# Moving DVE's two memory products ahead of the four masked score blocks in every attention tile

## Chip, cores and metric

One NeuronCore of one Trainium2 chip runs the whole kernel. The metric is the device time of one execution in microseconds (us). The engines are named as in the profile: PE (TensorE, matrix products), DVE (VectorE), ACT (ScalarE), POOL (GpSimd) and SP (SyncE, which issues DMAs).

## What is computed

The input is x, 4 batches of 1024 tokens by 256 features. After a layer norm the output is x + attention(xn) + ffn(xn). The feed-forward part is a mixture of 8 experts with two chosen for each token, plus a shared one. The attention has 16 heads of width 16 and mixes two things: causal linear attention inside the sequence, and four "fine" memories with learned norms.

```python
sq = elu1(q); M = fine_memories.sum(0); z = fine_memory_norms.sum(0)
out_coarse = (sq @ M) / clip(sq @ z, EPS)
a_f = einsum('bhsd,mhde->mbhse', sq, fine_memories)
n_f = einsum('bhsd,mhd->mbhs', sq, fine_memory_norms)
w = softmax(n_f.mean(-1), axis=0)
out_fine = (a_f / clip(n_f, EPS) * w).sum(0)
exp_prob = sigmoid(relu(coarse_repr @ eg_w1.T + eg_b1) @ eg_w2.T + eg_b2)
memory_output = exp_prob * out_fine + (1 - exp_prob) * out_coarse
# local_output, in chunks of 128 tokens, with carried S and z:
scores = einsum('bhid,bhjd->bhij', qc, kc) * mask
num = scores @ vc + qc @ S;  den = scores.sum(-1) + qc @ z;  out = num / clip(den, EPS)
output = gate * memory_output + (1 - gate) * local_output;  y = output @ w_o.T
```

## The kernel before

The kernel runs three phases one after the other. A tokens phase does the layer norm, the shared feed-forward part and the routing. An experts phase runs the chosen experts. The attention phase, from about 415 us to the end, works through 32 tiles of 128 tokens: 8 tiles t = 0 to 7 in each of 4 batches b = 1 to 4. A tile is written (b,t) below.

The order of the work in the attention phase is written out by hand in `attention_order()`, as one list of steps (name, b, t, j). Each engine walks the same list and does only its own share of each step. The engines meet through semaphores. `since(engine, semaphore, count)` is a wait, and `then_inc` is a signal at the end of an instruction.

The steps of a tile, in the order of the list, with the lines that do them:

- `scores` 0 to 3: PE multiplies keys and queries of four heads for each block (L1385, issued two blocks at a time). DVE multiplies each block with the causal mask into `probs` (L1632). The block's PSUM bank is free when DVE has read it.
- `fine` 0 and 1, for tile t-1: DVE multiplies half of the memory outputs `with_mem` with their coefficients `coef` into `prod`, which the profile calls `mem_rows` (L1670). POOL then adds the four memories and `rest` up into `att` (L1721 to L1725). PE has no part in it.
- `coarseT`: PE transposes the coarse output (L1402), ACT copies it (L1511).
- `keys`: PE transposes the keys (L1376), ACT copies them (L1496).
- `hidden`: PE (L1407), then ACT (L1515). `oproj` of tile t-2: PE multiplies with w_o (L1397), DVE adds it to `total` (L1678).
- `norms` 0 to 2, for tile t+1: PE multiplies the queries with the memories (L1370, three banks). ACT copies each bank into `with_mem` (L1490), where it waits until DVE's `fine` of tile t-1 has read the same buffer. DVE makes `rn` (L1620, L1622) and `coarse` (L1625) from it.
- `values`: PE multiplies all four blocks of `probs` with the values (L1416), ACT copies the result to `valT` (L1518).
- `gate` (L1433, ACT L1522), `state` (L1438), `local` (L1423, L1428): PE. DVE then makes `den` (L1638, L1640), the local output (L1641), `coef` and `rest` (L1646 to L1658), and folds the state (L1662).
- `outT` of tile t-1: PE transposes `att` (L1393), ACT copies it (L1499) and scales the rows that POOL gathered for the experts (L1506).

"Fill" steps lie between these: the projections q, k and v and the input transposes `xT` of later tiles and of the next batch (PE L88 to L90 and L1345, ACT L1476 to L1485, DVE L1557 to L1580). Which fill stands where depends on t. In tiles t = 0, 4, 5, 6 and 7 of the first three batches (t = 0 in all four) one stands ahead of `hidden`. For t = 2 `v` fills stand ahead of and behind `values`, for t = 1 and 3 one stands behind it; t = 7 also has an `xT` fill ahead of `values`. The tiles t = 4 to 7 of the last batch have no fills.

PE's results go to seven PSUM banks that are used in turn, the ring `a_ring` (`NR = 7`). Every step that writes a bank takes the next one. `use_bank` makes PE wait until the reader of the use seven before has finished. The steps `fine`, `rest`, `fold`, `state`, `split`, `mexp` and `weights` take no ring bank. SP issues the DMAs that lay queries and keys out in `q_st` and `k_st`. These wait for the scores that still read the old content.

Of the kernel before, what the change touches and what calls it, by code (L numbers as in the profile page):

```python
# [1073 lines left out]
def attention_order():  # L1074
    order = [("xT", 1, 1, 0), ("xT", 1, 1, 1)] + [("norms", 1, 0, j) for j in range(NB3)]
    order += [("q", 1, 1, 0), ("q", 1, 1, 1)]
    tiles = [(b, t) for b in range(1, B + 1) for t in range(NT)]
    for i, (b, t) in enumerate(tiles):
        fill = {0: [("k", b, 1, 0), ("split", b, 1, 0), None, ("k", b, 1, 1), ("split", b, 1, 1)],
                1: [None, None, ("v", b, 4, 0)],  # L1080
                2: [None, ("v", b, 5, 0), ("v", b, 6, 0)],
                3: [None, None, ("v", b, 7, 0)]}.get(t, [])
        if b < B:
            a = b + 1
            fill = {3: [None, None, ("v", b, 7, 0), ("xT", a, 0, 0), ("xT", a, 0, 1)],
                    4: [("q", a, 0, 0), ("q", a, 0, 1), ("split", a, 0, 0), ("k", a, 0, 0), None],
                    5: [("k", a, 0, 1), ("split", a, 0, 1), ("v", a, 0, 0)],
                    6: [("v", a, 1, 0), ("v", a, 2, 0), ("v", a, 3, 0)],
                    7: [("xT", a, 1, 0), ("xT", a, 1, 1), None, ("q", a, 1, 0), ("q", a, 1, 1)]}.get(t, fill)
        more = fill + [None] * 5  # L1090
        order += [("scores", b, t, 0), ("scores", b, t, 1)]
        if i:
            order.append(("fine", *tiles[i - 1], 0))
        order += [("coarseT", b, t, 0), ("scores", b, t, 2), ("scores", b, t, 3)]
        if i:
            order.append(("fine", *tiles[i - 1], 1))
        if t == 0:
            order.append(("mean", b, 0, 0))
        order += [("keys", b, t, 0), more[0], ("hidden", b, t, 0)]
        if i > 1:  # L1100
            order.append(("oproj", *tiles[i - 2], 0))
        if i + 1 < len(tiles):
            order += [("norms", *tiles[i + 1], j) for j in range(NB3)]
        if t == 0:
            order.append(("mexp", b, 0, 0))
        order += [more[1], ("values", b, t, 0), more[2], ("gate", b, t, 0)]
        if t < NT - 1:
            order.append(("state", b, t, 0))
        if t == 0:
            order.append(("weights", b, 0, 0))  # L1110
        order += [("local", b, t, 0), ("rest", b, t, 0)]
        if t < NT - 1:
            order.append(("fold", b, t, 0))
        order += more[3:5]
        if i:
            order.append(("outT", *tiles[i - 1], 0))
    order += [("fine", B, NT - 1, 0), ("fine", B, NT - 1, 1), ("oproj", B, NT - 2, 0), ("outT", B, NT - 1, 0),
              ("oproj", B, NT - 1, 0)]
    return [x for x in order if x]


ATT_ORDER = attention_order()

NR = 7
# [714 lines left out]
```

How the kernel before makes its waits and increments, by code:

```python
    def link(ins):  # L98
        links[0] += 1
        ins.then_inc(done, 1)
        eng.wait_ge(done, before + links[0])
# [140 lines left out]
        @block.sync  # L242
# [1 line left out]
            def tokens(u, index):  # L244
                sp.dma_start(x_in[u][:, :, :], x_tok[bass.ds(index, 1), :, :, :]
                             .rearrange("b p t c -> p (b t) c")).then_inc(s_x[u], 16)
            def tails():
                sp.wait_ge(s_tail, 1)
                for e in range(E):
                    at = sp.value_load(tail_i[0:1, e:e + 1], min_val=0, max_val=E * REGION - P)
                    sp.dma_start(d["rows"][bass.ds(at, P), :], filler).then_inc(s_tailed, 16)
            sp.wait_ge(s_x[0], 16)
            tokens(0, 0)
            sp.dma_start(st_g, d["sg_t"].rearrange("(k p) n -> p k n", p=P)).then_inc(s_sw, 16)
            sp.dma_start(st_u, d["su_t"].rearrange("(k p) n -> p k n", p=P)).then_inc(s_sw, 16)
            sp.dma_start(st_d[:, 0:2, :], d["sd_t"][0:2 * P, :].rearrange("(f p) n -> p f n", p=P)
                         ).then_inc(s_sw, 16)
            sp.dma_start(st_d[0:SF[2], 2, :], d["sd_t"][2 * P:FS, :]).then_inc(s_sw, 16)
            for it in range(B // 2):
                for u in range(2):
                    b = it * 2 + (2 + u)
                    sp.wait_ge(s_base, b * 2 * NS)
                    if b == B + 1:
                        sp.wait_ge(s_xst[0], 32)
                        for k in range(KC):
```

## Time and profile before

| | us |
|---|---|
| median of 3 runs | 847.85 |
| lowest and highest run | 846.88, 850.22 |
| the profiled execution | 844.33 |
| its span | 842.4 |
| its granted PE clock, mean | 0.924 |

The span runs from the first to the last instruction of the profiled execution. The granted clock is 1.0 at 2.4 GHz and 0.5 at 1.2 GHz. Busy time of PE is that of pipelined matrix products whose ends are modelled, so it isn't peak use. An idle time in a row is that of the engine just before the instruction, with the operation that ended it. "PEld" rows are PE's weight loads, which run beside its products.

### The profile page before, as it was taken

How to read it: one execution, taken by the hardware profiler on the slowest of the kernel's cores; microseconds unless marked ns; L12 is line 12 of the kernel's file. 1: busy time of each engine (PE TensorE's matmuls, PEld its weight loads, DVE VectorE, ACT ScalarE, POOL GpSimd, SP SyncE). 2: the span in 40 equal slices, each digit the busy share in tenths (PEclk: the TensorE clock that was granted, in tenths of full speed). 3: DMA queues.
4: the chain of work that ended last, by engine and by line, in shares of the span. 5: the costliest groups of instructions: out<-in, count | busy, mean ns of one | idle time of the engine just before them, and what ended most of it. 6: DMA issues, size and time to landing. Idle time of an engine off the chain costs nothing.

```text
span 842.4 us, 17283 instructions
## 1 busy us (share of the span) xinstructions
PE 672.4 (80%) x5154; PEld 566.1 (67%) x5155; DVE 561.4 (67%) x1353; ACT 356.4 (42%) x841; POOL 354.3 (42%) x438
## 2 busy tenths in 40 slices
PE   0689887980696999999678898878988888979884
PEld 0567766770685888888656776767866777757762
DVE  1475574674553555565467788878887788786883
ACT  0654453432332334333433464444644445454441
POOL 1043535355397400000233565355553655435663
PEclk9999999995798999999867999989999899989996
DMA  8107173442484333333325436374473634627210
GB/s 241 50 32 256 68 231 127 159 147 98 138 195 123 94 106 106 100 105 103 97 88 91 111 72 145 106 145 95 80 152 95 144 90 85 154 47 147 73 51 26
DMA packets 79723, 96.27 MB, mean 114 GB/s; under 512 B 15852, under 2 KB 63180, under 8 KB 79660
## 3 DMA queue, kind: packets, MB, share of 16 engines
q1 hardware_dynamic: 69132, 74.93, 34.7%
q0 software_dynamic: 7680, 19.93, 8.3%
q10 hardware_dynamic: 2848, 0.61, 0.4%
q8 instruction: 34, 0.56, 0.3%
q14 instruction: 29, 0.24, 0.1%
HBM read 38.68 MB, written 31.59 MB: 83 GB/s over the span
## 4 chain that ended last, share of the span: by engine, by line
DVE 20%; PE 18%; issue 7%; ACT 4%; POOL 1%; DVEq 0%; ACTq 0%; POOLq 0%
DVE probs L1632 4%; PE a_ring L88 2%; PE a_ring L1397 2%; PE a_ring L1416 2%; DVE mem_rows L1670 2%; PE a_ring L90 2%; PE a_ring L89 2%; PE a_ring L1428 2%; PE a_ring L1370 2%; DVE rest L1654 1%; DVE mem_rows L1641 1%; ACT with_mem L1490 1%; PE a_ring L1407 1%; DVE rn L1622 1%; PE a_sums L1438 1%
## 5 line engine op out<-in xcount | busy, mean ns | idle before, releaser
L1632 DVE TENSOR_TENSOR probs<-a_ring,causal 128x512 f32<-128x512 f32 x128 | 81.6, 677 | 0.6 <-DVE skT L1580 0.6
L1711 POOL TENSOR_TENSOR yg<-yg 128x256 f32<-128x256 f32 x32 | 25.5, 796 | 130.9 <-ACT yg L1506 130.9
L1490 ACT ACTIVATE with_mem<-a_ring 128x510 f32<-128x510 f32 (+1 forms) x96 | 46.0, 550 | 72.7 <-DVE mem_rows L1670 60.2
L1697 POOL DMA_INDIRECT yg<-d_grouped_y,from_row x64 | 63.3, 989 | 14.3 <-issue 10.2
L88 PE MATMUL e_up<-wb,xb 128*128 x144 | 54.3, 377 | 17.2 <-issue 16.7
L999 DVE TENSOR_TENSOR h_sb<-e_up,silu 128x176 f32<-128x176 f32 x72 | 24.5, 341 | 62.6 <-ACT silu L948 62.6
L1685 POOL MEMSET q_st<- 32x4096 f32 x2 | 7.0, 3504 | 130.0 <-POOLq L794 129.9
L1721 POOL TENSOR_TENSOR mem_rows<-mem_rows 128x512 f32<-128x512 f32 x32 | 42.2, 1317 | 45.5 <-DVE mem_rows L1670 45.4
L88 PE MATMUL e_y<-wd,hb 88*128 x146 | 49.0, 336 | 8.9 <-DVE hb L1006 7.7
L1397 PE MATMUL a_ring<-wo,attT 128*128 128x256 f32 x128 | 42.4, 459 | 12.5 <-DVE probs L1632 11.3
L953 ACT ACTIVATE hb<-e_h 88x256 fp32r<-88x256 f32 x72 | 27.4, 380 | 56.5 <-PE e_h L926 56.5
L780 POOL DMA_INDIRECT d_rows<-sqT,slot_i x32 | 33.2, 1039 | 42.2 <-DMA d_rows<-sqT,slot_i 36.8
L1370 PE MATMUL a_ring<-mem_st,q_st 128*128 128x170 f32 x256 | 48.6, 327 | 1.0 <-DVE probs L1632 0.4
L948 ACT ACTIVATE silu<-e_up 128x176 f32<-128x176 f32 x72 | 22.8, 316 | 59.5 <-PE e_up L90 59.5
L89 PE MATMUL e_up<-wb,xb 128*128 x144 | 47.7, 331 | 0.0
L90 PE MATMUL e_up<-wb,xb 128*128 x144 | 47.6, 330 | 0.0
L1385 PE MATMUL a_ring<-q_st,k_st 48*128 48x128 f32 x512 | 42.4, 284 | 3.9 <-DVE a_xT L1567 3.9
L780 POOL DMA_INDIRECT d_rows<-v,slot_i x32 | 33.7, 1053 | 27.4 <-DMA d_rows<-v,slot_i 19.8
L1370 PEld LDWEIGHTS a_ring<-mem_st,q_st 128*128 128x128 f32 x256 | 40.0, 217 | 6.6 <-DVE probs L1632 4.2
L1670 DVE TENSOR_TENSOR mem_rows<-with_mem,coef 128x512 f32<-128x512 f32 x64 | 44.1, 690 | 0.0
L1385 PEld LDWEIGHTS a_ring<-q_st,k_st 48*128 48x128 f32 x512 | 33.4, 186 | 15.4 <-issue 15.4
L88 PEld LDWEIGHTS e_up<-wb,xb 128*128 128x128 f32 x144 | 28.1, 195 | 22.0 <-issue 21.9
(308 smaller groups left out, 2164.7 us busy)
## 6 DMA issues: line engine op xcount, KB each, us to landing
q_st<-q_part SPq DMA_DIRECT2D x168, 64.0 KB
k_st<-k_part SPq DMA_DIRECT2D x168, 64.0 KB
xg<-d_rows SPq DMA_DIRECT2D x77, 128.0 KB, 2.0
d_grouped_y<-y_sb SPq DMA_DIRECT2D x73, 128.0 KB, 1.7
d_base<-xn_in SPq DMA_DIRECT2D x8, 512.0 KB, 3.6
xn_in<-d_xn SPq DMA_DIRECT2D x4, 1024.0 KB, 6.2
total<-d_base SPq DMA_DIRECT2D x8, 512.0 KB, 4.2
out<-total SPq DMA_DIRECT2D x8, 512.0 KB, 3.6
```

The source lines that it names most:

```text
L88: pe.matmul(out, a[0], b[0], start=start, stop=False)
L89: pe.matmul(out, a[0], b[1], start=False, stop=False)
L90: return pe.matmul(out, a[1], b[0], start=False, stop=stop)
L780: pool.indirect_dma_start(d["rows"], bass.IndirectOffsetOnAxis(ap=slot_i[u][:, k, t:t + 1], axis=0), xn[u][:, t, :], None).then_inc(s_sc[u ...
L1370: mm = pe.matmul(ps[:, i * WN:(i + 1) * WN], st["q"][t // TS][:, g, col], mem_st[:, g, :], start=True, stop=True)
L1385: mm = pe.matmul(two[r][:, i * P:(i + 1) * P], st["k"][t // TS][rows, g, col], st["q"][t // TS][rows, g, col], start=True, stop=True)
L1397: mm = pe.matmul(ps[:, 0:H], attT[t % 2][:, m, :], c["wo"][:, m, :], start=(m == 0), stop=(m == KC - 1))
L1490: act.activation(with_mem[t % 2][:, j * BP:j * BP + g, :], ps[:, 0:g * WN].rearrange("p (g w) -> p g w", g=g), ACT.Copy).then_inc(s_with, 1)
L1632: dve.tensor_tensor(probs[:, j, :, :], ps[:, :].rearrange("p (h i) -> p h i", i=P), c["causal"][:, :].unsqueeze(1).broadcast_to([P, 4, P]) ...
L1670: dve.tensor_tensor(prod[:, half, :, :].rearrange("p g n (r e) -> p g (n r) e", e=HD), with_mem[t % 2][:, half, 0:CF].rearrange("p g (m e) ...
L1697: pool.indirect_dma_start(yg[tile % GATHERS][:, k, :], None, d["grouped_y"], bass.IndirectOffsetOnAxis(ap=c["from"][:, k, tile:tile + 1], ...
L1721: link(pool.tensor_tensor(part[:, :, :, :], prod[:, :, 0:2, :], prod[:, :, 2:4, :], ALU.add))
```

## The change

In the hand-written order, the two `fine` steps of tile t-1 now stand ahead of tile t's score blocks. Before, `fine` 0 stood behind score block 1, and `fine` 1 behind score block 3. DVE's order at the start of a tile was scores 0, scores 1, fine 0, scores 2, scores 3, fine 1, and is now fine 0, fine 1, scores 0, 1, 2, 3. This holds for 31 of the 32 tiles; the first has no `fine` in front of it. PE and ACT have nothing to do for `fine`, and POOL's own steps keep their order among each other.

```diff
         more = fill + [None] * 5
+        if i:
+            order += [("fine", *tiles[i - 1], 0), ("fine", *tiles[i - 1], 1)]
         order += [("scores", b, t, 0), ("scores", b, t, 1)]
-        if i:
-            order.append(("fine", *tiles[i - 1], 0))
         order += [("coarseT", b, t, 0), ("scores", b, t, 2), ("scores", b, t, 3)]
-        if i:
-            order.append(("fine", *tiles[i - 1], 1))
         if t == 0:
             order.append(("mean", b, 0, 0))
         order += [("keys", b, t, 0), more[0], ("hidden", b, t, 0)]
```

## Rows read from the trace of the kernel before

**Rows 1.** The page, part 1: busy time of each engine
```profile
PE 672.4 (80%) x5154; PEld 566.1 (67%) x5155; DVE 561.4 (67%) x1353; ACT 356.4 (42%) x841; POOL 354.3 (42%) x438
```

**Rows 2.** The waits: who waited for whom, total, times, longest
```profile
DVE rn L1620 <- ACT with_mem L1490: 31.6, 31, 1.6
...
DVE den L1638 <- PE a_ring L1428: 21.3, 16, 2.3
```

**Rows 3.** The chain that ended last, around tile (3,3): start us, us, length, what
```profile
679.62 1.21 DVE probs L1632 x2
...
680.87 1.08 PE a_ring L1416 x32
```

**Rows 4.** Timeline of tile (3,3): start, length, engine, line, form, idle before
```profile
677.75 1.27 DVE L1632 TENSOR_TENSOR probs<-a_ring,causal 128x512 f32<-128x512 f32 x2
...
678.47 0.73 PEld L1397 LDWEIGHTS a_ring<-wo,attT 128*128 128x128 f32 x4 [1.21 <-DVE probs L1632]
...
679.23 0.85 PEld L1370 LDWEIGHTS a_ring<-mem_st,q_st 128*128 128x128 f32 x6
...
680.27 0.30 PEld L1370 LDWEIGHTS a_ring<-mem_st,q_st 128*128 128x128 f32 x2 [0.19 <-DVE probs L1632]
...
681.50 1.43 ACT L1490 ACTIVATE with_mem<-a_ring 128x510 f32<-128x510 f32 x3 [3.60 <-DVE mem_rows L1670]
...
684.01 0.98 PEld L1428 LDWEIGHTS a_ring<-ident,valT 128*128 128x128 f32 x8
...
685.17 0.17 DVE L1638 SCALAR_TENSOR_TENSOR den<-a_ring,over_keep 128x16 f32<-128x16 f32 x1 [0.38 <-PE a_ring L1428]
```

**Rows 5.** Timeline of tile (2,6), with a fill ahead of its hidden layer
```profile
612.25 1.28 DVE L1632 TENSOR_TENSOR probs<-a_ring,causal 128x512 f32<-128x512 f32 x2
...
612.98 0.65 PE L1407 MATMUL a_ring<-coarseT,w 128*64 128x128 f32 x4 [2.15 <-DVE probs L1632]
...
620.82 0.17 DVE L1638 SCALAR_TENSOR_TENSOR den<-a_ring,over_keep 128x16 f32<-128x16 f32 x1 [1.51 <-PE a_ring L1428]
```

**Rows 6.** Timeline of tiles (2,5), (3,4) and (4,4), where DVE didn't wait for the local products
```profile
606.72 0.97 PEld L1428 LDWEIGHTS a_ring<-ident,valT 128*128 128x128 f32 x8
...
608.66 0.16 DVE L1638 SCALAR_TENSOR_TENSOR den<-a_ring,over_keep 128x16 f32<-128x16 f32 x1
...
691.44 0.73 PEld L1397 LDWEIGHTS a_ring<-wo,attT 128*128 128x128 f32 x4 [0.17 <-DVE probs L1632]
...
796.21 0.97 PEld L1428 LDWEIGHTS a_ring<-ident,valT 128*128 128x128 f32 x8 [0.29 <-ACT valT L1518]
...
797.42 0.17 DVE L1638 SCALAR_TENSOR_TENSOR den<-a_ring,over_keep 128x16 f32<-128x16 f32 x1
```

**Rows 7.** Timeline of tiles (3,0) and (3,1): PE after its long waits
```profile
637.60 1.28 DVE L1632 TENSOR_TENSOR probs<-a_ring,causal 128x512 f32<-128x512 f32 x2
...
637.82 0.60 PE L1364 MATMUL a_ring<-norm_bd,qmean 128*128 128x32 f32 x4 [1.52 <-DVE qmean L1588]
...
638.41 0.19 PEld L88 LDWEIGHTS a_ring<-a_xT,wqkv 128*128 128x128 f32 x1
...
654.15 1.28 DVE L1632 TENSOR_TENSOR probs<-a_ring,causal 128x512 f32<-128x512 f32 x2
...
655.47 1.36 PEld L1397 LDWEIGHTS a_ring<-wo,attT 128*128 128x128 f32 x4 [0.33 <-DVE probs L1632]
```

**Rows 8.** PE by stretch: length, busy, (instructions), granted clock, DMA share, GB/s
```profile
462.00:465.00 3.00, 3.00 (x14) 0.51 0.58 137
...
612.00:615.00 3.00, 2.02 (x13) 1.00 0.78 186
...
639.00:642.00 3.00, 3.00 (x10) 0.50 0.23 63
```

**Rows 9.** Timeline: `den` of tiles (1,2) and (3,2)
```profile
469.71 0.17 DVE L1638 SCALAR_TENSOR_TENSOR den<-a_ring,over_keep 128x16 f32<-128x16 f32 x1 [2.27 <-PE a_ring L1428]
...
674.83 0.17 DVE L1638 SCALAR_TENSOR_TENSOR den<-a_ring,over_keep 128x16 f32<-128x16 f32 x1 [1.27 <-PE a_ring L1428]
```

## The prediction

> **What bounds the kernel now.** The page's busy times come first: PE is busy for 80% of the span, DVE for 67%, and neither is full [rows 1]. A second view is needed, the waits. They show what DVE waits for in the attention part: `den` waits for PE's local products (L1428) in 16 of 32 tiles, and `rn` waits for ACT's `with_mem` in 31 [rows 2]. Which wait is worth something isn't told there. The chain of waits says which of them sets the end. Around tile (3,3) it runs over DVE's masked scores 2 and 3, straight into PE's value products L1416, and on to L1428 and `den` [rows 3]. The second memory product of the tile before ("fine 1") stands behind score block 3 and isn't in it: today it lies beside PE's work.
>
> The timeline gives the loop in full. I count from the start of score block 0, T = 677.75 [rows 4]. Six DVE operations stand here, two of them fine. One follows the other after 0.60 us (blocks 2 and 3 take 1.21 on the chain [rows 3]), and a waiting PE starts 0.72 after the start of the block it waits for (678.47 - 677.75). The ring explains what PE waits for: seven banks, so a use waits for the reader of the seventh use before it. In this tile oproj needs block 0's bank, norms 0 block 1's, norms 2 block 2's, and values block 3's. Hence oproj at T+0.72 after 1.21 us of waiting, norms at T+1.48, a pause for block 2 to T+2.52, values at T+3.12. From there PE has no pause to L1428 (T+6.26), and `den` follows at T+7.42 after a wait of 0.38 [rows 3, 4].
>
> **The change, step by step.** Nothing is removed or added: 31 tiles have two DVE instructions moved, 62 in all. They issue no DMA. PE and ACT have no step for them. POOL keeps its order; it only may add up earlier. SP's queue is passed by nothing. So the cost or gain is all in who waits for whom.
>
> After the change, both fines run at T and T+0.60, and blocks 0 to 3 start at T+1.20, 1.80, 2.40, 3.00. They are released at T+1.92, 2.52, 3.12, 3.72. Blocks 0 and 1 are 1.20 later, blocks 2 and 3 are 0.60 later, and DVE has done all six at the same time as before. The fines add no wait of their own: their coefficients come from DVE's own preceding step, and `rest` of tile t-1 has already waited for the attention sum of t-2.
>
> PE in tile (3,3): oproj at T+1.92, norms 0.76 behind (679.23 - 678.47) at T+2.68. The six first loads take 0.85 [rows 4], so the eight take about 1.15 and end at T+3.83. Block 2's bank has been free since 3.12, so that pause is gone. Values start at T+3.84, against 3.12: +0.72. The loop gets longer by this, since all up to `den` is continuous PE work. What I expect is not the 1.20 of block 0 nor the 0.60 of block 3, but between them.
>
> What is given back: `with_mem` waits 3.60 for fine 1 [rows 4], which will be done by T+1.3. Its copies then wait for norms instead. The copy can start some 0.7 behind the first norms load, at T+3.4, and end at T+4.83 (1.43 later) against 5.18 now. DVE's `rn` comes 0.35 sooner, but in a tile where `den` waits for PE this only lengthens the wait for `den`. The same holds for POOL, whose `att` sum can start earlier: nobody waits for that sum, because PE's transposes of `att` stand behind L1428 in PE's queue.
>
> The tiles by their fills (t within the batch), each worked like (3,3):
> - t = 2: same ring, `v` fill in place of values waits for block 3. +0.71, four tiles: 2.8.
> - t = 3: +0.73, four tiles: 2.9.
> - t = 6: a fill ahead moves the ring by one, so the hidden layer waits for block 0 and oproj for block 1. PE's wait of 2.15 before hidden (at T+0.73) becomes 3.34; 0.14 comes back where norms 2 no longer pauses. `den` waited 1.51, so no slack [rows 5]. +1.05, three tiles: 3.2.
> - t = 4: a `q` fill of PE work stands before hidden and covers the wait: oproj, which needs block 1, has waited only 0.17 when it starts [rows 6], by when DVE has also done block 2. Nothing, three tiles. Without that cover it would cost 0.7 as in t = 3, 2 in all.
> - t = 5: the ring of t = 6, but DVE reaches `den` without waiting. PE's local products come 1.0 later, as in t = 6; `den` can then start at 606.72 + 1.0 + 1.16 = 608.88 against 608.66 [rows 6] (1.16 is L1428 to `den` in rows 4): +0.2, three tiles: 0.6.
> - t = 4 to 6 of batch 4, no fills: PE waits 0.29 for ACT's `valT` before L1428, and `den` stands 1.21 behind it without a wait [rows 6], 0.05 more than the 1.16. `valT` comes earlier with `with_mem`, so of PE's 0.72 these 0.34 are cover: +0.3 to 0.4, I take 0.3, three tiles: 0.9.
> - t = 1: PE is at half clock and starts oproj at T+1.32 [rows 7] (T = 654.15), after block 0's release. It moves to T+1.92: +0.60, four tiles: 2.4.
> - t = 0 of batches 2 to 4: the `k` fill needs block 0 and starts at T+0.81 [rows 7] (T = 637.60), so +1.11 at most; if the clock returns at its present time the later work runs faster and some +0.2 remains. I take 0.6, three tiles: 1.8.
> - t = 7: +0.3 in three batches (the same slack, then the `xT` fill): 0.9. The last tile has no norms, its values wait for block 3 alone: +0.6.
>
> The sum is 16.1 us. Its lower bound is 9.6: only the 0.60 by which block 3 is later, in the 16 tiles where `den` waits. Its upper bound is 17.6 (t = 0 at 1.11).
>
> **The clock.** The second term is PE's granted clock. Before block 0's release PE idles 1.21 in a tile like (3,3) [rows 4], and this becomes 2.4. In tile (3,0) the clock fell to half (0.50) behind an idle time of 1.52 [rows 7, 8]; a 2.15 idle in tile (2,6) left it at 1.00 [rows 5, 8]. In tile (1,2), whose head has the usual idle time, it fell too (0.51 [rows 8]), and `den` waited 2.27, against 1.27 in (3,2) [rows 9]: one fall costs 1.0 where part of PE's slow work still lay under waits. At half clock the four oproj loads take 1.36 against 0.73 [rows 4, 7]. After the change oproj and norms are wholly in the loop (1.91 us at full clock, some 1.6 more at half), so a fall costs 1.0 to 1.6; I take 1.3. Eighteen heads get 2.3 us or more of idle time (t = 2, 3 of four batches, t = 6, 7 of three, t = 4 to 7 of the last). No row shows such a head often enough for a rate. Between none and all, and nearer to tile (3,0) (2.3 is past 1.52) than to the usual head, I take ten: 13 us; bounds 0 and 18 x 1.6 = 29.
> The Trainium skill, TensorE: Matmul & The Clock Gate, section "HAM oscillation — how this bites in real kernels", says that PE pauses between bursts, among them those that come from cycling through PSUM banks, make the clock fall and rise again and again, each time at a cost. By that rule most of the eighteen heads would fall, more than my ten; the fall in tile (1,2) behind a wait on the ring agrees with it.
>
> **Forecast.** 16.1 + 13.0 = 29.1. The profiled execution took 844.33 (span 842.4) and gives 873.4. The profiled one is 3.5 below the median of the three runs shown, 847.85 (846.88 to 850.22), so the median becomes 877.
>
> **Rivals.**
> - The clock stays as it is: the sum alone, 847.85 + 16.1 = 864. For it: the 2.15 of idle time in (2,6) at full clock. Against: the fall in (1,2) behind the usual wait.
> - Only block 3's delay counts, since PE catches up on oproj and norms: 847.85 + 9.6 = 857. Against: the loads already follow each other without a pause.
> - Faster: `rn` is what counts. DVE waits for `with_mem` in 31 tiles, 31.6 us, behind fine 1 [rows 2]. If DVE's own sequence were the bound in all, 0.35 x 31 = 11 would be gained: 837. It decides where `den` doesn't wait for PE, and only while norms keep their place; both fail here, as norms are held by block 0's bank.
> - No change: the delay lies wholly in slack, 848. That needs 0.7 us of slack before `den`; 16 tiles have none.
> - Every head falls: 847.85 + 16.1 + 18 x 1.3 = 887, up to 893 at 1.6 each. For it: (3,0) fell behind 1.52 only. Against: (2,6). It is where the skill's rule above points.
>
> **Chances.** Longer loop and more falls 0.60; longer loop alone 0.22; block 3 alone 0.08; every head 0.04; faster 0.03; no change 0.03. A measurement of this kernel tells 0.5% (4 us) from nothing. Slower 0.94, same 0.03, faster 0.03. The range 857 to 891 takes in the first three cases.
>
> **What would show it.** In the profile after: the idle time of L1397 behind `probs` near 2.4 in tile (3,3)'s successors (3.3 of L1407 at t = 6); no pause between the norms loads; L1416 at 2.6 behind the start of block 0; ACT's wait for `mem_rows` gone, one for PE's L1370 in its place; `den`'s wait from 21.3 to some 40 us or more. The clock term stands or falls with the share of the attention part below full clock, which should grow at tile heads outside the batch boundaries. It is wrong if the distance between heads of t = 2 and 3 stays near 11.3, or if `den` stops waiting.

## The result, and the profile after

The changed kernel takes 910.0 us (median of 4 runs, 904.4 to 912.8) against 848.1 before: ratio 1.072 with a 95% interval of 1.066 to 1.078. That is 62 us slower. The forecast was 877, with a range up to 891: the direction was right, the size less than half of what came.

The page of the kernel after (busy times as in [rows 1], then the granted clock of PE in 40 slices of the span):

```profile
span 910.0 us, 17283 instructions
...
PE 709.2 (78%) x5154; PEld 600.0 (66%) x5155; DVE 568.7 (63%) x1353; ACT 362.0 (40%) x841; POOL 368.4 (40%) x438
...
PEclk9999998985988999996789997789887998878776
```

DVE has the same instructions and is busy only 7 us longer; PE is busy 37 us longer with the same instructions. From the twentieth slice on, 15 of the 21 slices of the clock row have an 8, a 7 or a 6 (7 of 21 in the page of the kernel before). So part of the loss is waiting, and part is PE working slower.

Who waited for whom, after:

```profile
ACT with_mem L1488 <- PE a_ring L1368: 80.1, 30, 4.6
DVE den L1636 <- PE a_ring L1426: 65.8, 25, 5.8
...
DVE rn L1618 <- ACT with_mem L1488: 37.8, 27, 1.8
PEld a_ring L1395 <- DVE probs L1630: 37.2, 24, 2.6
```

`den` waits for PE's local products 65.8 us in 25 tiles, where it was 21.3 in 16 [rows 2]. ACT's `with_mem` no longer waits for fine 1 at all and waits 80.1 us for the norms. These two turned out as forecast.

Tile (3,3) after, to be set beside [rows 4]. The lines have moved by two: L1395 is oproj, L1368 norms, L1414 values, L1426 local products, L1668 the fines, L1630 the masked scores:

```profile
711.97 1.46 DVE L1668 TENSOR_TENSOR mem_rows<-with_mem,coef 128x512 f32<-128x512 f32 x2
...
713.35 2.47 DVE L1630 TENSOR_TENSOR probs<-a_ring,causal 128x512 f32<-128x512 f32 x4
714.08 0.73 PEld L1395 LDWEIGHTS a_ring<-wo,attT 128*128 128x128 f32 x4 [2.58 <-DVE probs L1630]
...
714.83 2.00 PEld L1368 LDWEIGHTS a_ring<-mem_st,q_st 128*128 128x128 f32 x8
...
716.02 1.58 ACT L1488 ACTIVATE with_mem<-a_ring 128x510 f32<-128x510 f32 x3 [3.88 <-PE a_ring L1368]
...
716.98 1.42 PEld L1414 LDWEIGHTS a_ring<-probs,v 128*32 128x32 f32 x32 [0.15 <-issue]
...
720.74 0.98 PEld L1426 LDWEIGHTS a_ring<-ident,valT 128*128 128x128 f32 x8
...
721.89 0.17 DVE L1636 SCALAR_TENSOR_TENSOR den<-a_ring,over_keep 128x16 f32<-128x16 f32 x1 [2.90 <-PE a_ring L1426]
```

The idle time before oproj is 2.58, not 1.21. The norms loads now run without a pause, but eight of them take 2.00 us, where six took 0.85. `den` comes 9.92 us after the tile's start (721.89 - 711.97) and not 7.42. The chain of waits of the same stretch shows where these microseconds stand:

```profile
713.42 0.61 DVE probs L1630
...
714.08 1.34 PE a_ring L1395 x4
715.42 1.63 PE a_ring L1368 x8
717.05 1.62 PE a_ring L1414 x32
```

oproj and norms were not on the chain before [rows 3]; now they are on it whole. The four oproj loads still took 0.73, as at full clock; the norms loads took 2.00, at half clock. The granted clock, after, for the attention part, for two stretches around this head and for tile (1,2):

```profile
434.80:893.50 458.70, 379.03 (x3136) 0.83 0.41 87
710.00:714.00 4.00, 1.74 (x16) 1.00 0.69 150
714.50:717.50 3.00, 3.00 (x24) 0.56 0.34 98
465.00:477.00 12.00, 9.72 (x101) 1.00 0.59 116
```

And the attention part of the kernel before:

```profile
433.50:825.50 392.00, 342.20 (x3134) 0.94 0.47 101
```

At 710 to 714 the clock is full and PE is busy 1.74 of 4 us; just behind, it is near half. The fall begins behind the oproj loads. Over the attention part the mean is 0.83 in 458.7 us, where it was 0.94 in 392.0. A clock of 0.5 is half speed, so the time at half clock is 2 x 0.17 x 458.7 = 156 us against 2 x 0.06 x 392 = 47.

A tile after which kept full clock shows the other part by itself. This is (1,2):

```profile
465.23 1.46 DVE L1668 TENSOR_TENSOR mem_rows<-with_mem,coef 128x512 f32<-128x512 f32 x2
...
467.34 0.73 PEld L1395 LDWEIGHTS a_ring<-wo,attT 128*128 128x128 f32 x4 [2.52 <-DVE probs L1630]
...
468.09 1.08 PEld L1368 LDWEIGHTS a_ring<-mem_st,q_st 128*128 128x128 f32 x8
...
469.13 0.19 PEld L88 LDWEIGHTS a_ring<-wqkv,a_xT 128*128 128x128 f32 x1
...
473.19 0.98 PEld L1426 LDWEIGHTS a_ring<-ident,valT 128*128 128x128 f32 x8
...
474.35 0.17 DVE L1636 SCALAR_TENSOR_TENSOR den<-a_ring,over_keep 128x16 f32<-128x16 f32 x1 [2.24 <-PE a_ring L1426]
```

oproj at T+2.11, the `v` fill at T+3.90 (it was T+3.12), `den` at T+9.12. The tile is 12.04 long. Before, (3,2), a tile of the same kind at full clock, was 11.26 long with `den` at T+8.34.

### The profile page after: what moved, and what is told of

Same layout as the page of the kernel before. It is cut to its first block, busy times and chain, and to the rows that moved or that the text cites. A ratio compares the mean times of both kernels' runs of the same rounds, so it can differ in the third digit from the quotient of the medians.

```text
span 910.0 us, 17283 instructions
## 1 busy us (share of the span) xinstructions
PE 709.2 (78%) x5154; PEld 600.0 (66%) x5155; DVE 568.7 (63%) x1353; ACT 362.0 (40%) x841; POOL 368.4 (40%) x438
## 4 chain that ended last, share of the span: by engine, by line
PE 27%; DVE 17%; issue 6%; ACT 2%; POOL 0%; DVEq 0%; POOLq 0%; ACTq 0%
PE a_ring L1395 5%; PE a_ring L1368 4%; DVE mem_rows L1668 4%; PE a_ring L1414 4%; PE a_ring L1426 3%; PE a_ring L88 3%; DVE probs L1630 2%; PE a_ring L89 2%; PE a_ring L90 2%; PE a_sums L1436 2%; PE a_ring L1421 2%; DVE rest L1652 1%; DVE mem_rows L1639 1%; PE a_ring L1405 1%; DVE state L1660 1%
## 5 line engine op out<-in xcount | busy, mean ns | idle before, releaser
L1709 POOL TENSOR_TENSOR yg<-yg 128x256 f32<-128x256 f32 x32 | 26.8, 836 | 207.0 <-ACT yg L1504 207.0
L1488 ACT ACTIVATE with_mem<-a_ring 128x510 f32<-128x510 f32 (+1 forms) x96 | 47.4, 549 | 80.7 <-PE a_ring L1368 80.1
L1630 DVE TENSOR_TENSOR probs<-a_ring,causal 128x512 f32<-128x512 f32 x128 | 79.0, 675 | 0.0
L1395 PE MATMUL a_ring<-wo,attT 128*128 128x256 f32 x128 | 53.0, 555 | 32.3 <-DVE probs L1630 31.2
L1695 POOL DMA_INDIRECT yg<-d_grouped_y,from_row x64 | 67.3, 1051 | 14.4 <-issue 10.2
L1395 PEld LDWEIGHTS a_ring<-wo,attT 128*128 128x128 f32 x128 | 30.4, 262 | 44.7 <-DVE probs L1630 37.2
L1368 PE MATMUL a_ring<-mem_st,q_st 128*128 128x170 f32 x256 | 55.8, 379 | 1.6 <-DVE probs L1630 1.6
L1368 PEld LDWEIGHTS a_ring<-mem_st,q_st 128*128 128x128 f32 x256 | 49.3, 270 | 6.1 <-DVE probs L1630 2.0
L1668 DVE TENSOR_TENSOR mem_rows<-with_mem,coef 128x512 f32<-128x512 f32 x64 | 51.8, 847 | 0.4
L1405 PE MATMUL a_ring<-coarseT,w 128*64 128x128 f32 x128 | 25.5, 332 | 32.3 <-DVE probs L1630 20.7
L1636 DVE SCALAR_TENSOR_TENSOR den<-a_ring,over_keep 128x16 f32<-128x16 f32 x32 | 5.6, 174 | 66.0 <-PE a_ring L1426 65.8
```

What stands on the lines that cost most here:

```text
L1368: mm = pe.matmul(ps[:, i * WN:(i + 1) * WN], st["q"][t // TS][:, g, col], mem_st[:, g, :], start=True, stop=True)
L1395: mm = pe.matmul(ps[:, 0:H], attT[t % 2][:, m, :], c["wo"][:, m, :], start=(m == 0), stop=(m == KC - 1))
L1488: act.activation(with_mem[t % 2][:, j * BP:j * BP + g, :], ps[:, 0:g * WN].rearrange("p (g w) -> p g w", g=g), ACT.Copy).then_inc(s_with, 1)
L1630: dve.tensor_tensor(probs[:, j, :, :], ps[:, :].rearrange("p (h i) -> p h i", i=P), c["causal"][:, :].unsqueeze(1).broadcast_to([P, 4, P]) ...
L1668: dve.tensor_tensor(prod[:, half, :, :].rearrange("p g n (r e) -> p g (n r) e", e=HD), with_mem[t % 2][:, half, 0:CF].rearrange("p g (m e) ...
L1695: pool.indirect_dma_start(yg[tile % GATHERS][:, k, :], None, d["grouped_y"], bass.IndirectOffsetOnAxis(ap=c["from"][:, k, tile:tile + 1], ...
```

## The experiments

Two theories stood against each other. Theory A: the loop of DVE's scores, PE and `den` got longer by the 16 us of my sum, and the rest is PE's clock, which falls when PE has nothing but a wait at the head of a tile (each drop to half clock is called a fall). Theory B: the low clock is a by-product, and the later release of the banks costs the whole.

Tiles are compared below by their length, from the start of its six DVE operations to the start of the next tile's. The lengths of tiles are read from the profiled execution of each kernel. The kernel before was timed again in each series of experiments, with medians of 848.0 to 850.6 us, and each ratio is against its own series.

**e1: constant products in PE's waiting time.** The changed kernel plus:

```diff
+WARM = {(b, t): 8 for b in range(1, B + 1) for t in range(NT) if t in (1, 2, 3, 6, 7) or b == B and t >= 4}
...
                     ps = use_bank(pe, item) if what != "state" else sums
+                    if what == "keys" and (b, t) in WARM:
+                        for _ in range(WARM[b, t]):
+                            pe.matmul(ps[:, :], w["wqkv"][0][:, 0:P], w["wqkv"][0][:, 0:512], start=True, stop=True)
```

> The changed kernel, with 8 products of constant weights (128x512, result thrown away) put into PE's queue ahead of the keys' transposes in 18 tiles: t = 1, 2, 3, 6, 7 of every batch and t = 4, 5 of the last, 22 tiles in all. They lie in the time in which PE only waits for block 0. Theory A (PE's waiting at the head of a tile makes its clock fall, and the falls are the larger part of the loss): the falls go, the longer loop of 16 us stays, some 864 us (858 to 874). Theory B (the falls are a by-product and the later release of the banks is the loss): as the changed kernel, 905 to 915, or a little more for the added work.

The tiles treated are 22: t = 1, 2, 3, 6, 7 of each batch and t = 4, 5 of the last.

Measured: 881.3 us (874.2 to 882.4), ratio 1.038 (1.036 to 1.041), outside the range that theory A gave. Work was added, and the kernel became 29 us faster. The products in the profile of e1, at the head of tile (3,2):

```profile
683.14 2.12 PE L1343 MATMUL a_ring<-wqkv 128*128 128x512 f32 x8
685.10 0.38 PE L1378 MATMUL a_ring<-ident,skT 128*128 128x128 f32 x2
685.41 0.65 PE L1409 MATMUL a_ring<-coarseT,w 128*64 128x128 f32 x4
686.53 1.13 PE L1399 MATMUL a_ring<-wo,attT 128*128 128x256 f32 x4 [0.47 <-DVE probs L1634]
```

They fill 683.14 to 685.26, keys and hidden follow, and oproj waits 0.47 instead of 2.35. In the profiled execution (at 874.2 the fastest of the five) the tiles at t = 2, 3, 6 and 7 of the first three batches all keep full clock, and are 12.06, 12.05, 12.62 and 13.88 long. The changed kernel had 13.6 to 14.7 (12.04 in (1,2)), 13.6, 14.2 and 15.3 to 15.5. Theory B falls with this. Of the miss of 17 us against the 864, some 8 is the loop, which is longer than the 16 us put in (e5 and e7 below). In the profiled execution the rest lies at the batch boundaries, where tile t = 0 still takes 19.1 instead of 16.6 with more time at half clock than before the change, and in (1,1) and (1,4). The other four executions took 5.7 to 8.2 us more than the profiled one; they have no trace.

**e8: three products instead of eight**, the only edit `8 for` to `3 for`.

> As e1 with 3 constant products in place of 8 in the same tiles, so that PE's idle time at the heads is about 1.7 us instead of 0.5 and of the changed kernel's 2.5, near that of e3 (1.8). Theory A: a part of the falls comes back, between e1 and the changed kernel, 885 to 900 us. If the products act otherwise than by filling the wait (each one the same): three eighths of e1's gain, 899 us.

Measured: 874.1 us (868.2 to 874.7), 1.030 (1.025 to 1.034). Both numbers of mine were wrong: three products do as much as eight or more. In the profiles of e1 and e8, both at 874, the tiles t = 2, 3, 6 and 7 of batches 2 to 4 are as long to within 0.03 us. So the gain isn't in proportion to the added work, and a remaining wait of 1.5 to 1.8 us at these heads is harmless here, while 2.3 to 2.6 was not.

**e3: one fine ahead of the scores.** In the order of the list:

```diff
+        if i:
+            order.append(("fine", *tiles[i - 1], 0))
         order += [("scores", b, t, 0), ("scores", b, t, 1)]
-        if i:
-            order.append(("fine", *tiles[i - 1], 0))
```

> Order fine 0, scores 0, 1, 2, 3, fine 1: blocks 0 and 1 are released 0.60 later than in the kernel before, blocks 2 and 3 as there. The loop itself grows by some 4 us (0.1 at t = 2 and 3, 0.45 at t = 6, 0.5 at the batch boundaries). PE's wait at the head is 1.8 instead of 1.2. Theory A: falls in part of the heads, 1.7 each, 858 to 880 us. If the clock doesn't answer to 0.6 more of idle time: 852 us.

Measured: 865.4 us (864.0 to 866.1), 1.019 (1.017 to 1.022), inside the range of theory A. With full clock its tiles at t = 2, 3, 6 are 11.42, 11.43, 12.00 long (11.24, 11.13, 11.48 before). The tiles (2,2), (3,2), (4,2), reached behind a batch boundary, fell to half clock and took 14.3 to 14.4. (2,6) and (3,6) took 13.4, and t = 7 of the first three batches 14.9 instead of 13.9. The tiles t = 3 and the last batch from t = 3 to t = 6 kept full clock. So a delay of block 0 by one fine brings falls in 8 of the 24 tiles t = 2 to 7, where the change brought them in 19 and the kernel before had one, (1,2). PE's idle time at the head was 1.7 to 1.9 in tiles that fell and 1.7 in tiles that didn't.

**e2: fine 1 up, behind fine 0**, so that only blocks 2 and 3 are late (order: scores 0, 1, fine 0, 1, scores 2, 3).

> Order scores 0, scores 1, fine 0, fine 1, scores 2, scores 3: blocks 2 and 3 are 0.60 later as in the change, blocks 0 and 1 as before, so PE's wait at the head stays at 1.2 us. Theory A: +0.60 in the tiles whose local products are awaited, +0.3 in three of the last batch, 9 us in all, few new falls: 857 us (854 to 863). Theory B (the later block 3 is what costs, through whatever follows it): more than half of the change's loss, over 880 us.

Measured: 861.0 us (859.8 to 869.4), 1.018 (1.012 to 1.023). Tiles t = 2 and 3 are 11.86 and 11.73 long: +0.62 and +0.60, as expected for the last block's 0.60. The order with late blocks 2 and 3 costs 12 us (861.0 against 849.1 in its series). Not all of this is the loop: (1,4), (3,4) and (3,6), among others, fell, and took 15.0, 15.0 and 14.0 where the kernel before has 13.7, 13.7 and 11.5.

**e5: products at the batch boundaries too.** e1 with 8 ahead of the mean at t = 0, 12 ahead of the keys at t = 1 and at t = 6 of three batches, and the rest as in e1.

> The changed kernel with the constant products of e1 in more places: 8 ahead of the mean at t = 0, 12 ahead of the keys at t = 1 and at t = 6 of the first three batches, 8 at t = 2, 3, 7 and at t = 4 to 7 of the last batch. Theory A (PE's idle time at the heads and at the batch boundaries makes the clock fall, everything else is the loop): what is left is the longer loop, from e1's tiles at full clock 16 to 19 us, less what the kernel before itself loses by falls: 860 us (852 to 868), and hardly a stretch below full clock in the attention part. Theory B (e1's gain is not that of the clock): no better than e1, 875 to 882.

Measured: 862.3 us (858.2 to 866.5), 1.016 (1.011 to 1.021). The attention part is nearly at full clock (this execution is the slowest of the four; (1,1), (1,2), (2,1) and (2,4) still fell):

```profile
433.00:847.60 414.60, 383.92 (x3380) 0.97 0.45 96
```

**e7: the same at the boundaries of the kernel before** (8 ahead of the mean at t = 0, 12 ahead of the keys at t = 1, no other edit).

> The kernel before with constant products at the batch boundaries alone: 8 ahead of the mean at t = 0 and 12 ahead of the keys at t = 1. Theory A: its 44 us at half clock in the attention part are nearly all there, and each costs about 0.3 to 0.45: 837 us (832 to 843). Theory B: 849.

Measured: 838.7 us (835.5 to 844.7), 0.990 (0.987 to 0.993). Its attention part:

```profile
433.50:822.00 388.50, 352.72 (x3226) 0.98 0.47 103
```

e5 and e7 are the changed and the unchanged order with few falls in either. Their difference, 862.3 - 838.7 = 23.6 us, is the longer loop, to within the few falls that are left in both. The rest of the 62, some 38, is clock: falls cost the changed kernel 47.7 us (910.0 - 862.3) and the kernel before 9.4 (848.1 - 838.7).

**e12: POOL's additions cut short.** Fine 0 takes longer in its new place. POOL and DVE in the changed kernel, head of tile (1,3):

```profile
475.89 0.82 POOL L1709 TENSOR_TENSOR yg<-yg 128x256 f32<-128x256 f32 x1 [4.17 <-ACT yg L1504]
...
476.79 0.79 POOL L1710 TENSOR_TENSOR total<-total,yg 128x256 f32<-128x256 f32 x1
...
477.27 1.46 DVE L1668 TENSOR_TENSOR mem_rows<-with_mem,coef 128x512 f32<-128x512 f32 x2
```

Before, DVE did a masked score block here, which reads PSUM. To see whether POOL's additions (L1709, L1710) are the cause, e12 is e5 with these cut to one column, which leaves the expert rows out of nearly all of the output:

```diff
-link(pool.tensor_tensor(rows[:, 0, :], rows[:, 0, :], rows[:, 1, :], ALU.add))
+link(pool.tensor_tensor(rows[:, 0, 0:1], rows[:, 0, 0:1], rows[:, 1, 0:1], ALU.add))
-pool.tensor_tensor(total[:, t, :], total[:, t, :], rows[:, 0, :],
+pool.tensor_tensor(total[:, t, 0:1], total[:, t, 0:1], rows[:, 0, 0:1],
                    ALU.add).then_inc(s_ysum, 1)
```

> e5 with POOL's two additions of the expert rows cut to one column in every tile (the expert part is thereby left out of nearly all of the output). In the changed kernel fine 0 takes 0.8 to 0.86 us where it was 0.67, at a time when POOL adds the expert rows; in e4, where the fines stand last, they take 0.68. Theory (the fine step, moved to the tile's first place, meets POOL's additions, which read and write the same memory): the fines take 0.68 again, block 0 is released 0.15 to 0.19 sooner, and the tiles at t = 2 and 3 are that much shorter; with the rest step, which also lies beside these additions, up to 0.5 a tile, 850 us (845 to 858). Rival (fine 0 is long because of what precedes it on DVE): the fines keep 0.85 and the time stays at 862.

Measured: 841.6 us (840.9 to 841.8), ratio 0.990 (0.984 to 0.995), faster than the 845 to 858 that I expected. The fines, as shortest, median and longest in ns, in the changed kernel, e5 and e12:

```profile
L1668 DVE TENSOR_TENSOR mem_rows<-with_mem,coef x64: 676/855/1212, 450.6 to 897.2; 128x512 f32<-128x512 f32 x64
```

```profile
L1675 DVE TENSOR_TENSOR mem_rows<-with_mem,coef x64: 677/869/1215, 449.9 to 851.8; 128x512 f32<-128x512 f32 x64
```

```profile
L1675 DVE TENSOR_TENSOR mem_rows<-with_mem,coef x64: 677/685/711, 450.3 to 828.1; 128x512 f32<-128x512 f32 x64
```

They fall from 0.87 to 0.69 us, and t = 2 from 12.05 to 11.49. Not all of the 21 us belongs to the fines: `rest` (L1658 before), which meets the same additions in every version (0.62 us in the kernel before), drops from a mean of 0.68 to 0.43 as well. An estimate from the means: 64 fines x (0.85 - 0.69) = 11 us of DVE's time and 32 x (0.68 - 0.43) = 8 us in `rest`. The additions were not cut in the kernel before, so how much of the 21 us the change itself brought isn't shown; its fines took 0.69 on average with the additions in place. The Trainium skill, SBUF — State Buffer, section "Who interferes with whom", says that a DVE instruction with two SBUF inputs contends with a GpSimd instruction that reads SBUF. The runs agree: 0.69 us without POOL's additions, 0.87 with them.

**e4: both fines behind the scores** (order: scores 0, 1, 2, 3, fine 0, 1), the opposite of the change.

> Order scores 0 to 3, fine 0, fine 1: blocks 2 and 3 are released 0.60 earlier than in the kernel before, the fines end where they ended. PE doesn't pause for block 2, values start at T+2.65 instead of T+3.12. Theory A (the loop runs over the last block): 0.4 to 0.5 less in some 13 tiles, 842 us (838 to 846). Rival: ACT's with_mem and DVE's rn, which still wait for fine 1, take over, 848 us.

Measured: 844.3 us (843.5 to 845.4), 0.995 (0.993 to 0.996): faster, by half a per cent. PE's loads in tile (3,2) of e4, whose scores start at 667.91:

```profile
668.63 0.73 PEld L1397 LDWEIGHTS a_ring<-wo,attT 128*128 128x128 f32 x4 [1.20 <-DVE probs L1632]
669.39 1.08 PEld L1370 LDWEIGHTS a_ring<-mem_st,q_st 128*128 128x128 f32 x8
670.43 0.19 PEld L88 LDWEIGHTS a_ring<-wqkv,a_xT 128*128 128x128 f32 x1
```

The norms no longer pause for block 2, and the `v` fill begins at T+2.52 instead of T+3.12. Tile t = 2 is 10.64 long and t = 3 10.66, both 0.5 to 0.6 shorter. But (1,6), (2,6) and (3,6), which kept full clock before, fell and are 1.2 to 1.3 longer, although PE waits only 1.74 at their heads where it waited 2.15 before.

**e6: e4 with products where the clock falls** (8 at t = 0 ahead of the mean, 12 at t = 1, 8 at t = 6).

> The order of e4 (both fines behind the scores) with constant products ahead of the mean at t = 0 (8), of the keys at t = 1 (12) and at t = 6 (8). Theory A: e4's falls at t = 6 (1.9 us each, three) and those of the boundaries (3 or more us each, four) go: 832 us (826 to 839). Theory B: as e4, 844.

Measured: 831.5 us (829.1 to 832.7), 0.981 (0.978 to 0.984). This beats both kernels.

**e9, e10: real work as cover.** The `v` projections of some tiles move from behind norms and values to between keys and hidden: in e9 in the changed kernel for t = 1, 2, 3, in e10 in e6 for t = 2, 3.

```diff
+        ahead = [x for x in more[:3] if t in (1, 2, 3) and x and x[0] == "v"]
+        more = [None if x in ahead else x for x in more]
...
-        order += [("keys", b, t, 0), more[0], ("hidden", b, t, 0)]
+        order += [("keys", b, t, 0), *ahead, more[0], ("hidden", b, t, 0)]
```

> The changed kernel, and nothing added: the v projections of t = 1, 2 and 3, which stood behind norms and values, now stand between keys and hidden, as cover made of real work. Theory A: the pure wait of the heads at t = 2 and 3 shrinks from 2.5 to 1.8 us and fewer of them fall; at t = 3 the loop is some 0.5 shorter, at t = 2 and 1 it keeps its length. 895 us (885 to 905). Theory B (only the place of the banks in the ring counts, and the fills move it by one or two, so that more steps wait for later blocks): 910 us or more.

> e6 (both fines behind the scores, constant products at t = 0, 1, 6) with the v projections of t = 2 and 3 moved between keys and hidden. Theory A: two falls that e6 shows at t = 3 go (1.6 us each), and at t = 2 the loop is 0.4 to 0.6 shorter, four times: 827 us (823 to 832). If DVE's own sequence is already the bound in these tiles and the falls only move: 831.

Measured: e9 901.8 us (901.2 to 903.1), ratio 1.061 (1.055 to 1.067); e10 831.6 (829.9 to 834.4), 0.978 (0.972 to 0.984). e9 is 8 us better than the change, about half of the 15 expected but inside the range. The two were not timed in one series, and the intervals of their ratios just meet. e10 is no better than e6: its falls at t = 3 are gone, others stand at t = 4 (two tiles of 15.0) and in (3,7), and the one in (4,4) stayed.

**e11: e6 with three products in more places.**

> e6 with fewer products in more places: 3 ahead of the mean at t = 0 and of the keys at t = 2, 3, 6 and in the last batch's t = 4 to 7, 12 at t = 1. Theory A: e6's falls in (2,3), (3,3) and (4,4) go, 1.2 to 1.7 us each, and e8 has shown that 3 are enough at a head: 828 us (824 to 832). If 3 are too few at t = 0 and t = 6: 835.

Measured: 831.6 us (830.0 to 834.4), 0.978 (0.972 to 0.984). The falls in (2,3) and (3,3) are gone. But (2,4) and (3,4) fell instead (15.0 long), (4,4) fell as before, and t = 2 became 11.65 long instead of 10.89: there PE has no waiting time to spare, and the products stand in the loop. Three kernels that fill different places, e6, e10 and e11, end at 831.5.

## Why the prediction was wrong

The mechanism was right in its parts, and the direction with it. Two terms of the sum were too small.

**"Eighteen heads get 2.3 us or more of idle time ... I take ten: 13 us."** This is the step that failed. The term measured 38 us in the medians: 62 less the 23.6 of e5 against e7. The time at half clock grew by 109 us, from 47 to 156. The profiled executions, whose spans differ by 67.6 us (910.0 - 842.4), say where. Each tile was compared with the same tile at full clock in e1, e5 or e7. The falls in the tiles t = 2 to 7 cost 37.8 us after the change and 1.0 before; those at t = 0 and t = 1 cost 18.1 and 12.0. That is 43 us more by the clock, beside 23.4 for the loop and 1.3 ahead of the attention part. Four things in the term were wrong.
- The number. Seventeen of my eighteen heads fell, all but (1,2), and two others with them, (2,4) and (3,5). The rival "every head falls" had 0.04. I took the case against it from (2,6), which kept its clock behind 2.15 of idle time; yet in e4 the same tile fell behind 1.74. The rule of the Trainium skill that the prediction quotes pointed to this rival and was nearer to the trace than my ten. (What that page, TensorE: Matmul & The Clock Gate, says of pauses from cycling through PSUM banks stands in its section "A second HAM failure mode: psum-queue depth-cycling".)
- The batch boundaries. The term had no falls there beyond those of the kernel before. They cost 6 us more.
- The repetition. Some tiles spend 6.8 or 10.2 us at half clock ((2,2), (4,5)). My term counted one fall for each head. Why a second one followed in some tiles, while 13 of the 24 had one alone, isn't shown.
- The price. (3,3) is 13.62 long with one fall and 12.05 without (e5): 1.57, at the upper end of the "1.0 to 1.6; I take 1.3". The thirteen tiles with one fall lost 1.1 to 1.7, most of them 1.5 to 1.7. Beside the number of falls this is a small part.

**The sum of 16.1 for the loop** measured 23.6. Tile by tile, at full clock on both sides (e1 or e5 against the kernel before, for t = 0 and 1 against e7):

| tile | forecast | measured | tiles |
|---|---|---|---|
| t = 0 | 0.6 | 1.25 | 3 |
| t = 1 | 0.6 | 1.45 | 4 |
| t = 2 | 0.71 | 0.81 | 4 |
| t = 3 | 0.73 | 0.93 | 4 |
| t = 4 | 0 | 0.16 | 3 |
| t = 5 | 0.2 | 0.32 | 3 |
| t = 6 | 1.05 | 1.14 | 3 |
| t = 7 | 0.3 | 0.03 | 3 |
| (4,4) to (4,6) | 0.3 | 0.52 | 3 |
| (4,7) | 0.6 | 0.80 | 1 |

With their counts they make 23.8. For t = 1 the value is that of (3,1) and (4,1). For (4,7) it is the delay of `den`; the end of the kernel comes only 0.36 later, which makes the sum 23.4. "Both fines run at T and T+0.60" was the mis-sized step: beside POOL's additions block 0 starts at T+1.38, not T+1.20, in most tiles. It starts at T+1.64 at t = 4, at T+2.06 at t = 5, and at T+1.74 at t = 0 and 1. In e12, without the additions, it starts at T+1.20 in all of them (T+1.24 at t = 5). At t = 0 and t = 1 this is 0.54 of delay that the sum didn't have. There I also let the present falls cover part of the delay; without any fall these tiles lose 1.25 and 1.45. In (4,4) to (4,6) the cover of 0.34 was there: in e1 the values of (4,4) start 0.92 later than before and L1430 (L1428 before) only 0.56 later, without its wait for `valT`. What was missing is the same 0.18.

What held: oproj's idle time (2.5 to 2.6 against 2.4), no pause in the norms, the value products 2.65 behind the start of block 0 at full clock (e1 and e5; 2.64 forecast), `with_mem` waiting for L1368 in place of the fines, `den`'s wait over 40, and the cover at t = 4, (2,4) apart. The wait of 3.3 at t = 6 did not come. It was 2.2, since PE was itself later: in (2,6) its last work before the wait ended 1.4 ahead of the tile's start before the change, and 0.1 after it.

The rival "the clock stays as it is" had 864, and e5 measures 862.3. That the two agree is luck: the loop in that rival is 7.5 too short, and e5 also lacks the falls that cost the kernel before 9.4. With the measured loop the rival would be 848.1 + 23.6 = 872. "Faster: `rn` is what counts" is excluded: `rn` waits 37.8 us now, no less than before, since `with_mem` hangs on the norms.

What stays open is which head falls. e4, e8, e10 and e11 show the falls moving from tile to tile with small shifts of the timeline, and runs of one kernel differ by up to 9 us in e7. With longer idle time at the heads more of them fell: one of the tiles t = 2 to 7 before, 8 in e3, 19 after the change. But the added products fill idle time and are work as well, and no run tells these two apart. No run here gives a rule by which a single fall could be told beforehand. Not tried: a ring of more banks, which might loosen the loop itself.

## What to carry to other kernels

Where a ring of PSUM banks ties PE to the engine that empties it, put the operations that free banks ahead of those that don't; here the order scores first, memory products last was the better one (831.5 against 838.7 with the clock kept up in both). A delay of 0.6 us of the last blocks was paid in full at t = 2 and 3 (e2); one of the first block alone cost 0.2 and 0.3 there (e3). Cost the wait of PE twice, once as a wait and once by what the clock does afterwards, and count that second term for every place where the wait stands, not for a part of them: here it was the larger one, 38 us against 24. Before an operation with two SBUF inputs is moved, look at what POOL does at its new place.

## What the runs showed of the hardware

- A wait of PE of 2.2 to 2.6 us at the head of a tile was followed by half clock at 17 of 18 heads, and one such fall cost 1.57 us in (3,3), a tile with no slack. (1,2) kept full clock behind 2.52. A wait of 1.5 to 1.8 was followed by none in batches 2 to 4 of e8, and by falls in 8 tiles of e3 (1.7 to 1.9).
- Adding work made the kernel faster: 8 thrown-away products a tile gave 29 us in the changed kernel, 3 gave 36, and 20 at each batch boundary gave 9 us in the kernel before. Where PE had no wait to fill they made the tile longer: 11.65 instead of 10.89 at t = 2 (e11 against e6).
- A DVE product of two SBUF tensors, 128x512, takes 0.69 us (median) with POOL's additions cut to one column, and 0.87 with the 128x256 additions beside it (e12 against e5).
